# A fused attention and expert block on one core: four reordered products on TensorE and a reordered second norm on VectorE

## The reference

```python
x = x + attention(layernorm(x))      # shifted 7x7 windows, 12 heads of 8, bias and masks, softmax, projection
t = layernorm(x)
probs = softmax(t @ gate_w + gate_b) # 4 experts, the two best are kept and renormalised
h = gelu(t @ w1[e] + b1[e])          # 96 -> 384
y = h @ w2[e] + b2[e]                # 384 -> 96
x = x + sum_e gate[e] * y[e]
```

## Time and profile before

| | |
|---|---|
| median of 3 runs | 6502.03 us (6498.84 to 6503.11) |
| profiled execution, its own time | 6496.24 us |
| its span | 6494.4 us |
| mean granted TensorE clock | 0.996 of full |
| PE | 96% busy, 98560 matmuls |
| DVE | 78% busy |
| ACT | 73% busy |
| POOL | 58% busy |
| DMA queues | 14.5% and 0.9% of 16 engines |

### The profile page before, as it was taken

How to read it: one execution, slowest core, us unless ns; L and a number is a source line. 1 busy time by engine, 2 the same in 40 slices (tenths; PEclk the granted TensorE clock), 3 DMA queues, 4 the chain that set the end, 5 groups by cost and what they waited for, 6 DMA issues and landing times.

```text
span 6494.4 us, 263563 instructions
## 1 busy us (share of the span) xinstructions
PE 6253.5 (96%) x98560; PEld 5051.2 (78%) x98560; DVE 5075.3 (78%) x15911; ACT 4719.9 (73%) x9087; POOL 3756.6 (58%) x3337
## 2 busy tenths in 40 slices
PE   5999999999999999999999999999999999999998
PEld 4787777777877777778777777777777777777876
DVE  5777777777777777878787778777777777777775
ACT  3777777777777777777777777777777777777775
POOL 2565556555655565556555555655565556555655
PEclk9999999999999999999999999999999999999999
DMA  1111111111111111111111111111111111111110
GB/s 58 45 43 45 46 45 43 45 47 45 45 44 47 44 45 45 46 44 45 45 46 44 45 46 45 43 45 46 45 43 45 46 45 43 45 46 45 45 42 24
DMA packets 190610, 289.99 MB, mean 45 GB/s; under 512 B 42450, under 2 KB 151634, under 8 KB 189266
## 3 DMA queue, kind: packets, MB, share of 16 engines
q1 hardware_dynamic: 189394, 273.23, 14.5%
HBM read 138.18 MB, written 77.07 MB: 33 GB/s over the span
## 4 chain that ended last, share of the span: by engine, by line
PE 76%; DVE 13%; ACT 4%; issue 3%; POOL 3%; SPq 1%; DVEq 0%; DMA 0%; ACTq 0%; POOLq 0%
PE ps_t L1043 12%; PE ps_o L1060 10%; PE ps_f L971 8%; PE ps_f L972 8%; PE ps_f L973 8%; PE ps_s L1023 5%; PE ps_s L1033 4%; PE ps_f L1135 4%; PE ps_f L1137 4%; PE ps_f L1133 4%; POOL rstd L439 2%; PE ps_o L1069 2%; DVE stat L768 2%; PE ps_f L1075 2%; DVE xr L765 2%
## 5 line engine op out<-in xcount | busy, mean ns | idle before, releaser
L450 POOL TENSOR_TENSOR g_lo<-g_sb,g_hi 128x784 f16<-128x784 f32 x1152 | 2014.6, 1758 | 1749.0 <-DVE g_hi L880 1047.8
L543 ACT ACTIVATE g_sb<-ps_f 128x392 f32<-128x392 f32 x3072 | 1526.1, 497 | 109.4 <-PE ps_f L973 108.8
L565 ACT ACTIVATE pt_sb<-ps_t 113x588 f32<-113x588 f32 x1024 | 677.3, 661 | 1009.3 <-PE ps_t L1043 996.5
L737 DVE TENSOR_REDUCE s_max<-ps_s 113x12 f32<-113x588 f32 x1024 | 789.3, 771 | 616.3 <-PE ps_s L1033 616.3
L1137 PE MATMUL ps_f<-w_hi,g_lo 128*128 128x96 f16 x8832 | 1228.6, 206 | 0.0
L1135 PE MATMUL ps_f<-w_lo,g_hi 128*128 128x96 f16 x8832 | 1228.0, 206 | 0.0
L1133 PE MATMUL ps_f<-w_hi,g_hi 128*128 128x96 f16 x8832 | 1227.4, 206 | 0.0
L460 POOL TENSOR_TENSOR xr<-y_gated,xr 112x192 f32<-112x192 f32 (+1 forms) x1536 | 986.0, 659 | 323.1 <-DVE y_gated L898 224.1
L971 PE MATMUL ps_f<-x_hi,w_hi 128*128 128x392 f16 x3072 | 1012.3, 330 | 23.9 <-issue 9.5
L973 PE MATMUL ps_f<-x_hi,w_lo 128*128 128x392 f16 x3072 | 1011.0, 329 | 0.0
L972 PE MATMUL ps_f<-x_lo,w_hi 128*128 128x392 f16 x3072 | 1010.9, 329 | 0.0
(11 more groups left out here) (132 smaller groups left out, 13230.1 us busy)
## 6 DMA issues: line engine op xcount, KB each, us to landing
k_bd<-keys SPq DMA_DIRECT2D x1536, 36.8 KB
q_st<-qk_hi SPq DMA_DIRECT2D x768, 49.0 KB, 1.9
xr<-x SPq DMA_DIRECT2D x224, 139.1 KB
out<-xr SPq DMA_DIRECT2D x224, 139.1 KB
xa<-x SPq DMA_DIRECT2D x224, 136.5 KB
keys<-qk_hi SPq DMA_DIRECT2D x128, 147.0 KB, 2.1
keys<-qk_lo SPq DMA_DIRECT2D x128, 147.0 KB, 2.7
q_st<-qk_lo SPq DMA_DIRECT2D x384, 49.0 KB, 1.9
```

Source lines behind the costliest of these rows:

```text
L450: nc.gpsimd.tensor_tensor(g_lo[:, slot, 0:TOK], g_sb[:, chunk, :], g_hi[:, slot, 0:TOK], ALU.subtract).then_inc(lo_done, 1)
L543: nc.scalar.activation(g_sb[:, chunk, half * STRIP:(half + 1) * STRIP], h_bank[k % 3][:, 0:STRIP], ACT.Gelu, scale=1.0 / WSCALE).then_inc( ...
```

## The change

In PE's program: group 2 moves from behind the transposes of pair 0 to behind the scores of pair 1, ahead of those transposes. In pair 7 the transposes come before `qk(b, 0)`, not behind it. The values are made in two halves with the turn of pair 7 between them. Group 9 writes bank 0 instead of 4, so that group 11, which has bank 4, has no earlier group to wait for; group 9 itself gets a wait for the third `qk_low` of `b`, since `qk(b, 2)` lies in bank 0.

In ACT's program copy_pt(7) comes before `qk_high(b, 0)`.

In DVE's program `qk_low(b, 2)` moves from ahead of the residual to behind the variances of tiles 0 to 3, ahead of combine 8. Variances of 4 to 6 move up, directly behind their statistics; centre 0-3, scale 0-3 and centre 4-6 follow, and combine 9 moves from ahead of centre 0-3 to between centre 4-6 and scale 4-6.

No instruction is added or removed but for the one wait and the loss of another.

```diff
--- before.py
+++ after.py
@@ -114,7 +114,7 @@
 TURNS_AT_END = ((), (), (), (), (3,), (), (5,), (6,))
 X1_LOW_AT = ((), (), (), (), (), (0, 1), (2, 3), ())
 
-Y_BANK = (5, 7, 6, 5, 7, 6, 7, 7, 7, 4, 7, 4)
+Y_BANK = (5, 7, 6, 5, 7, 6, 7, 7, 7, 0, 7, 4)
 B2_COLS = EXPERTS * 3 * C
 
 N_T1, N_QK, N_V, N_S, N_PT, N_O, N_OT = 2, 4, 2, 8, 16, 8, 2
@@ -581,9 +581,9 @@
 
                 exps(a, 0)
                 for n in range(8):
+                    copy_pt(a, n)
                     if n == 7 and b is not None:
                         qk_high(b, 0)
-                    copy_pt(a, n)
                     if n < 7:
                         exps(a, n + 1)
                     if f is not None:
@@ -753,7 +753,7 @@
                                 s_rec[:, :].unsqueeze(2).broadcast_to([SPAN, HEADS, HD]), ALU.mult
                                 ).then_inc(onorm_done, 1)
 
-            def residual(f, before=None):
+            def residual(f, before=None, b=None):
 
                 u = f[1] % UPI
                 per = 16 * len(piece_list(u, SHIFT_OUT))
@@ -793,15 +793,17 @@
                 first_part, second_part = (0, 0, 4), (1, 4, 3)
                 sums_of(*first_part)
                 variances(*first_part)
+                if b is not None:
+                    qk_low(b, 2)
                 if before is not None:
                     combine(before, 8)
                 sums_of(*second_part)
+                variances(*second_part)
+                centre(*first_part)
+                scale(*first_part)
+                centre(*second_part)
                 if before is not None:
                     combine(before, 9)
-                centre(*first_part)
-                variances(*second_part)
-                scale(*first_part)
-                centre(*second_part)
                 scale(*second_part)
                 x2_low(f, 0)
                 if before is not None:
@@ -938,8 +940,7 @@
                 normalise_o(a, 7)
                 if b is not None:
                     qk_low(b, 1)
-                    qk_low(b, 2)
-                residual(a, f)
+                residual(a, f, b)
                 if b is not None:
                     qk_low(b, 3)
                 router_a(a)
@@ -1158,11 +1159,13 @@
                         experts(f, groups.pop(0))
                     if n < 7:
                         scores(a, n + 1)
+                    if n == 0 and groups:
+                        experts(f, groups.pop(0))
                     if n:
                         attend(a, n - 1)
+                    transpose_p(a, n)
                     if n == 7 and b is not None:
                         qk(b, 0)
-                    transpose_p(a, n)
                     for m in TURNS_BEHIND_P[n]:
                         turn_o(a, m)
                     if n == T1_AT and b is not None:
@@ -1178,13 +1181,18 @@
                     qk(b, 1)
                 attend(a, 7)
                 if b is not None:
-                    values(b)
+                    values(b, (0,))
                 turn_o(a, 7)
+                if b is not None:
+                    values(b, (1,))
                 if b is not None:
                     qk(b, 2)
                 project(a)
                 if f is not None:
                     for g in LATE_GROUPS:
+                        if Y_BANK[g] == 0 and b is not None:
+
+                            pe.wait_ge(qklo_done, at(b, N_QK, 3))
                         experts(f, g)
                 transpose2(a, b)
                 hidden(a, (0,))
```

## The result

The changed kernel takes 6554.36 us (median of 4 runs, 6552.25 to 6556.06) against 6500.43 us for the kernel before (6497.79 to 6503.11): a ratio of 1.0085, 95% interval 1.0073 to 1.0097. The change makes it 54 us slower, where 42 us were forecast (6542, range 6498 to 6580).

A forecast was written before the change was run, and what follows sets the result against it. PE, busy 96% of the span, was taken as the bound, so only its holds could matter. Terms 0.09 - 0.32 + 0.56 = +0.33 us a unit, times 126 = +42 us on 6502, 6544, given as 6542; range 6498 to 6580.

The forecast's parts named there:

- Third group: Pair 0, group 2 ahead of the transposes: the 0.37 hold only moves to before attend(0); +0.09 us a unit.
- First key product and values: Pair 7 to projection: attend(7) 0.27 earlier, new hold of some 0.2 before the turn, projection earlier; -0.32 us a unit.
- Late part: Projection to second transposes: group 9 held 0.90 for the third low part, replacing 0.35 before group 11; +0.56 us a unit.
- Behind the transposes: From the second transposes to hidden(0), 1.88 us: nothing changes, costed at nothing.
- Group 9 is not held: Rival at group 9: third low part ready in time, 0.35 hold gone; -0.58 us a unit, 6429 us; chance 0.05.
- copy early: Rival in pair 0: copy ends before scores of pair 2, 0.37 won; -0.13 us a unit, 6486 us; chance 0.06.
- The rival of a slower outcome: Second norm: DVE's path later than PE's, pair 7 gains only 0.15; +0.80 us a unit, 6603 us; chance 0.08.
- The figure of the Trainium skill: Group 8's 28 matmuls: about 81 ns each, 2.27 us in all, so group 9's new wait would cost nothing.

The follow-up runs named there:

- The late part alone: Kernel before with group 9 in bank 0 and its wait, third qk_low later, variances 4-6 earlier, combine 9 later: 6558.19 us, ratio 1.0089.
- the third group alone: Kernel before with only group 2 moved ahead of the transposes of pair 0: 6506.73 us, ratio 1.0014.
- the last kernel: Changed kernel with group 9 in bank 4 again, without its wait for the third low part: 6892.45 us, ratio 1.0606.

## Why the prediction was right, and where its sum was off

**Third group.** As put: the hold moves from the transposes to attend(0). The prediction had +0.09 with a range of 0 to 0.10. The trace shows 5.95 us again, and the attend itself takes 0.04 longer (3048.50 to 3049.16 for 3020.85 to 3021.47), so +0.04, or 5 us, by the trace; the 9 us of the runs are the same within their interval.

**First key product and values.** This is the term that was mis-sized: -0.32, with bounds of -0.56 to -0.15, and it is +0.02, outside them. The mechanism was named, the normalisation being late for the turn, and so was its time (1.35 from attend(7) to the turn; 1.36 measured). Four durations were put too low. Attend(7) comes 1.88 behind the transposes and not 1.77. The turn, started out of a wait, takes 0.23 and not 0.11; the prediction's own rows have 0.14 for a turn without a wait, and a turn that had waited took 0.24 in the kernel before, the next row starting at 3032.58:

```profile
3032.34 0.13 PEld L1069 LDWEIGHTS ps_o<-turn,o_tok 113*96 113x96 f32 x1 [0.26 <-DVE o_tok L752]
```

The second half of the values takes 0.62 for 0.56, and the product behind it 0.54 for 0.50. Together 0.33. The experiments part them: pair 7 gives -0.17 us a unit, the split takes +0.18 back before the projection. I had treated the two as one edit and so missed that one of them was a loss.

**Late part.** As put: group 9 is held until the third low part is made, 0.90 in the place of 0.35, and DVE's path is close behind PE's: its scaling ends at 3078.24 (3077.68 + 0.56), and the second transposes start at 3078.39. Forecast +0.56 at the second transposes, with bounds of +0.45 and +0.75, measured +0.39, outside them too. Some 0.09 is the projection, which takes 1.36 and not 1.45 when PE comes to it without a wait: the residual sum starts 0.97 behind its start for 1.06, and group 9 stands nearer by as much. (Two readings on that way are off by 0.07 and cancel: from the sum to the low part it is 1.88 for 1.95, from the low part's end to group 9 0.13 for 0.06.) Another 0.10 is group 11, 1.27 without a wait in front of it for the 1.37 that I took from a row with one. The late part alone, which has only the second, gives +0.48 there.

**Behind the transposes.** "Nothing changes" was nearly right: hidden(0) follows 1.84 behind them for 1.88.

So the sum was 0.04 + 0.02 + 0.39 - 0.04 = 0.41 and not 0.33, 52 us for 42. Two errors of opposite sign, +0.34 and -0.17, and two small ones. The direction was no luck, since the late part alone costs 60 us, but the closeness of the number was in part. With the first error alone the sum would be 0.67 a unit, 84 us, which is above the range.

**The rivals.** "Group 9 is not held" and "copy early" are excluded by the waits and by the third group alone. The rival of a slower outcome with DVE's path as the later one did not happen, but that path is within 0.15 of deciding. The figure of the Trainium skill that the prediction weighed ("TensorE: Matmul & The Clock Gate", section "Back-to-back issue gap") does not fit the changed kernel either: the 28 matmuls of its group 8 start between 3073.23 and 3074.46, 0.046 apart, and PE then waits for the low part.

What stays open: why the product ahead of attend(7) takes 0.59 with the copy made, and what makes the clock fall in one unit of the last kernel and not in the next. Neither was tried by itself.

## What to carry to other kernels

A short wait of the bounding engine is worth only the distance to the next path that ends there: removing the 0.35 before group 11 gave nothing until 0.26 was taken out of the other engine's chain. Before an operation goes down a queue to free its old place, look whether that place was idle: in the kernel before, the third low part stood in time in which DVE waited anyway, and moving it cost 0.48 on one path and 0.90 on the other. A block cut in two to advance something must leave a first half that still covers the latency behind it, and each restart of PE costs as well.

## What the runs showed that I had not expected

A turn that starts out of a wait takes 0.23 to 0.24 us and one that does not 0.09 to 0.14, the projection takes 1.36 without and 1.45 with a wait ahead of it, and an attend 0.66 out of a wait for 0.62. Small holds cost more than their length.

The changed kernel has a hold of 0.90 us in each unit and a mean granted clock of 0.995 to 0.996, where the kernel before has 0.994 to 0.996. With 2.20 us of idle time in each unit the clock fell to half in 93 of 127 units, and this cost some 120 of the 338 us. The same hold in the other units left it at full.
